# Softmax and squared-attention sums in a four-block transformer kernel: where their inverses are taken, and when statistics, sums and outputs are due

## What is computed

```python
x = x + squared_attention(_layernorm(x), Wq, Wk, Wv, Wo, gamma, beta)   # "squared"
x = x + gated_attention(_layernorm(x), W_gate, W_qkv)                   # "gated"
x = x + mqa_attention(_layernorm(x), Wqkv_w, Wqkv_b, out_w, out_b)      # "mqa"
x = x + gated_attention(_layernorm(x), W_gate, W_qkv)                   # "gated"
```

## Time and profile before

| | us |
|---|---|
| time before, median of 3 runs | 4368.68 (4368.31 to 4374.84) |
| the profiled execution's own time | 4371.04 |
| its span, first to last instruction | 4369.3 |
| PE busy | 3769.0 |
| POOL busy | 2965.8 |
| DVE busy | 1880.1 |
| ACT busy | 1638.2 |

### The profile page before, as it was taken

The page is one execution under the profiler, slowest core; times in us unless marked ns, Lnnn a source line. Parts: engine busy times, 40 slices in busy tenths (PEclk is TensorE's granted clock), DMA queues, the critical chain, the costliest instruction groups (busy, mean ns, idle before and its releaser), DMA issues. The chain is left out here.

```text
span 4369.3 us, 67371 instructions
## 1 busy us (share of the span) xinstructions
PE 3769.0 (86%) x26082; PEld 1520.9 (35%) x26082; DVE 1880.1 (43%) x4874; ACT 1638.2 (37%) x2433; POOL 2965.8 (68%) x2207
## 2 busy tenths in 40 slices
PE   7898998986989899898878878888898898998986
PEld 5343434332433333333333332333333333333332
DVE  1222222222555455455454444444454455555552
ACT  1544544552143333333434333333323333333343
POOL 2888787894076766767777666675565657666687
PEclk8999999998999999999999999999999999999998
DMA  1000100012010100101010010000100101000001
GB/s 68 15 15 22 37 20 30 11 59 73 10 30 1 59 1 23 37 1 40 20 32 28 11 37 13 27 32 15 44 1 15 44 1 59 1 23 27 1 29 40
DMA packets 63385, 115.08 MB, mean 26 GB/s; under 512 B 8673, under 2 KB 9185, under 8 KB 63073
## 3 DMA queue, kind: packets, MB, share of 16 engines
q1 hardware_dynamic: 63072, 110.77, 7.9%
HBM read 77.19 MB, written 33.55 MB: 25 GB/s over the span
## 5 line engine op out<-in xcount | busy, mean ns | idle before, releaser
L866 ACT ACTIVATE probs_soft<-banks 128x1024 f32<-128x1024 f32 (+1 forms) x960 | 848.3, 935 | 1339.8 <-PE banks L1171 1335.4
L774 POOL TENSOR_TENSOR added_soft<-added_soft,probs_soft 128x512 f32<-128x512 f32 (+1 forms) x380 | 1151.8, 3031 | 18.5 <-POOL added_soft L767 3.2
L959 DVE CUSTOM_DVE_ANT_0 banks<-banks,mask 128x128 f32<-128x128 f32 (+3 forms) x1536 | 701.3, 527 | 682.9 <-PE banks L1186 682.9
L954 DVE TENSOR_REDUCE maxima_soft<-banks 128x2 f32<-128x1024 f32 x384 | 452.4, 1221 | 503.3 <-PE banks L1186 503.3
L751 POOL TENSOR_SCALAR_AFFINE_SELECT probs_soft<-probs_soft 128x512 f32<-128x512 f32 x384 | 239.1, 635 | 568.6 <-ACT probs_soft L866 568.3
L1186 PE MATMUL banks<-k_soft,q_soft 32*128 32x512 f32 (+3 forms) x4608 | 508.8, 534 | 64.1 <-ACT probs_soft L866 63.6
L1139 PE MATMUL banks<-wide,xnT_soft 128*128 128x512 f32 x1024 | 500.6, 612 | 19.3 <-DVE picking_soft L938 11.0
L872 ACT ACTIVATE probs_squared<-banks,key_scale_squared 128x512 f32<-128x512 f32 (+3 forms) x768 | 378.9, 588 | 287.3 <-PE banks L1171 282.5
L1171 PE MATMUL banks<-q_soft,k_soft 32*128 32x512 f32 (+3 forms) x4608 | 481.2, 500 | 0.0
L1232 PE MATMUL banks<-probs_soft,v_soft 128*32 128x512 f32 (+3 forms) x4608 | 446.2, 507 | 10.2 <-DVE scaled_out_soft L1083 3.5
L774 POOL TENSOR_TENSOR added_squared<-added_squared,probs_squared 128x512 f32<-128x512 f32 (+1 forms) x124 | 376.9, 3039 | 5.1 <-POOL added_squared L774 1.4
(11 more groups left out here) (152 smaller groups left out, 4271.3 us busy)
## 6 DMA issues: line engine op xcount, KB each, us to landing
tiles_soft<-out SPq DMA_DIRECT2D x96, 256.0 KB, 2.7
rest_soft<-out SPq DMA_DIRECT2D x96, 256.0 KB, 2.9
out<-rest_soft SPq DMA_DIRECT2D x96, 256.0 KB, 2.1
tiles_squared<-in_x SPq DMA_DIRECT2D x32, 256.0 KB, 2.7
rest_squared<-in_x SPq DMA_DIRECT2D x32, 256.0 KB, 2.9
out<-rest_squared SPq DMA_DIRECT2D x32, 256.0 KB, 2.0
wide<-in_gated_wqkvT SPq DMA_DIRECT2D x3, 1024.0 KB, 7.7
raw_wq<-in_squared_wq SPq DMA_DIRECT2D x1, 1024.0 KB, 5.6
```

Of the source, the lines that this page charges most:

```text
L774: ins = pool.tensor_tensor(sums, sums, slot(ph, n)[:, :, col:col + width], ALU.add)
L866: ins = act.activation(slot(ph, n)[:, 2 * a:2 * a + 2, 0:width], score_pair(e, a)[:, :, 0:width], ACT.Exp, scale=SCALE)
L954: ins = dve.reduce_max(m["maxima"][:, ph % 2, 2 * a:2 * a + 2, t, p], score_pair(e, a)[:, :, col:col + width], AX_X)
L959: ins = dve.tensor_tensor_reduce(scores, scores, k["mask"][:, CHUNK - width:CHUNK], 1.0, MASKED, ALU.add, ALU.max, m["maxima"][:, ph % 2, ...
```

## The change

- `rs`, `widen` and `rw` go, and with them the transposes of sums and inverses. For gated and mqa phases VectorE takes reciprocals in place on `sums`, 128 columns at a time (`inv`, four for each chunk, in the half-steps after `sm`), and GpSimd multiplies 128x512 of `y` by them (`nrm`). Squared phases keep their `nrm` on VectorE.
- `out` of a gated stage no longer multiplies with inverses: VectorE adds the residual straight from PSUM, as in the other kinds; GpSimd's add goes. Every `out` now waits for `normalized`.
- `sm` comes one half-step later (16 and 10 instead of 15 and 9). Outputs 4 to 7 of a stage may not come before half-step 15, and the queue may pass over them.
- The statistics of the first four tiles of the next stage move from just before their `ln` in the stage's second phase into the projections of its first phase (`sprinkled`); those of tile t + 3 now come with `ln` of tile t. At most one `ln` is handed out in a half-step. The first four residual loads (`rload`), and for mqa the bias adds that go with them, move ahead of the next stage's tile loads.
- The mqa value bias is added by ScalarE as it evicts the products, not by VectorE later.
- The first four outputs of an act's last stage come one half-step later.

```diff
-SUMS_AT = (15, 9)
+SUMS_AT = (16, 10)
...
-        if t >= 2 and t + 2 < NT:
-            steps[-1].append(("stats", s, t + 2))
+        if t and t + 3 < NT:
+            steps[-1].append(("stats", s, t + 3))
...
+def sprinkled(work, some):
+
+    placed, first = list(work), len(work) // 3
+    for n in reversed(range(len(some))):
+        placed.insert(first + (len(work) - first) * n // len(some), some[n])
+    return placed
...
-    if kind == "gated":
-        return [(("rs", ph, c), 2)]
-    if kind == "mqa":
-        return [(("rs", ph, c), 2), (("widen", ph, c), 3), (("rw", ph, c), 4)]
+    if kind != "squared":
+
+        return [(("inv", ph, c, n), min(n + 1, 3 + c)) for n in range(TPC)] + [(("nrm", ph, c), 3 + c)]
     return [(("nrm", ph, c), 2)]
...
+    if event[0] == "out" and event[2] >= TPC:
+        return SUMS_AT[1] + 5
...
-        while queue and queue[0][1] <= n and (least * weight(queue[0][0], kinds) <= room or queue[0][2] <= n + 1):
-            room -= weight(queue[0][0], kinds)
-            events.append(queue.pop(0)[0])
-        carry = max(room, 0.0) if queue and queue[0][1] <= n else 0.0
+        while (x := due(queue, n)) is not None and (least * weight(queue[x][0], kinds) <= room or queue[x][2] <= n + 1):
+            if queue[x][0][0] == "ln" and normed:
+                break
+            normed = normed or queue[x][0][0] == "ln"
+            room -= weight(queue[x][0], kinds)
+            events.append(queue.pop(x)[0])
+        carry = max(room, 0.0) if due(queue, n) is not None else 0.0
...
+        head = ([("rload", s - 1, t) for t in range(TILES)] * (s > 0) + head[0], head[1])
...
-            work = [(head[0], 1), (parted(own[0]), HALVES - 2), (mixed(parted(outs[:half]), parted(own[1]), kinds), 2 * HALVES - 2)]
+            work = [(head[0], 1), (sprinkled(parted(own[0]), head[1]), HALVES - 2), (mixed(parted(outs[:half]), parted(own[1]), kinds), 2 * HALVES - 2)]
...
-            halves[-2] += parted(tail[:early])
-        work += [(head[1], 2 * HALVES - 2), (parted(merged), 2 * HALVES + 6), (parted(later + first), (3 if kinds[s + 1:s + 2] != ["squared"] else NG) * HALVES - 2),
+            halves[-1] += parted(tail[:early])
+        work += [(parted(merged), 2 * HALVES + 6), (parted(later + first), (3 if kinds[s + 1:s + 2] != ["squared"] else NG) * HALVES - 2),
...
+                elif u == "nrm" and soft:
+                    _, ph, c = e
+                    pool.wait_ge(sg.inverted, place["inv", ph, c, TPC - 1] + 1)
+                    wait_free(pool, ("av", ph, "AC"[c]))
+                    out = y_of(ph)[:, CHUNK * c:CHUNK * c + CHUNK]
+                    pool.tensor_tensor(out, out, m["sums"][:, c], ALU.mult).then_inc(sg.normalized, 1)
...
+                elif u == "inv":
+                    _, ph, c, n = e
+                    wait_free(dve, ("sm", ph, c))
+                    some = tile_of(m["sums"][:, c], n)
+                    dve.reciprocal(some, some).then_inc(sg.inverted, 1)
...
-                elif u == "rs":
-                    _, ph, c = e
-                    out = free(e)
-                    need(("sm", ph, c))
-                    for t in range(TPC):
-                        ins = pe.transpose(tile_of(out, t), tile_of(m["sums"][:, c], t), k["ident"][:])
-                    ready(e, ins)
-                elif u == "rw":
-                    _, ph, c = e
-                    out = free(e)
-                    pe.wait_ge(sg.widened, place["widen", ph, c] + 1)
-                    for t in range(TPC):
-                        ins = pe.transpose(tile_of(out, t), m["wide_inverse"][:, t].rearrange("p i d -> p (i d)"), k["ident"][:])
-                    ready(e, ins)
                 elif u == "out":
                     _, s, t = e
                     out = free(e)
                     for g in range(NG):
                         ph = NG * s + g
-                        if kind_of(s) == "gated":
-                            need(("av", ph, "AC"[t // TPC]))
-                        elif kind_of(s) == "mqa":
-                            need(("rw", ph, t // TPC))
-                        else:
-                            pe.wait_ge(sg.normalized, place["nrm", ph, t // TPC] + 1)
+                        pe.wait_ge(sg.normalized, place["nrm", ph, t // TPC] + 1)
```

More of the change, by code:

```diff
@@ L229, in mixed, with due @@
     return events
+def due(queue, n):
+    for x, (e, first, _) in enumerate(queue):
+        if first <= n:
+            return x
+        if "out" not in (e[0], e[1][0] if e[0] == "more" else ""):
+            return None
+    return None
 def spread(kinds, halves, rooms, work):
@@ L587, in act_program @@
     order = {name: [e for e in events if e[0] == name] for name in
-             ("load", "rload", "stats", "out", "mxr", "split", "krep", "vst", "ksq", "qsq", "kvar", "nrm", "rs", "widen", "rw", "gate")}
+             ("load", "rload", "stats", "out", "mxr", "split", "krep", "vst", "ksq", "qsq", "kvar", "inv", "nrm", "gate")}
     order["picks"] = [e for e in events if e[0] in ("kall", "vall")]
@@ L654, in stage_of @@
     def stage_of(e):
-        return e[1] // NG if e[0] in ("rs", "rw") else e[1]
+        return e[1]
     own_weights = OWN_WEIGHTS[soft]
@@ L709, in _ @@
                     _, s, t = e
-                    if kind_of(s) == "gated":
-                        sp.wait_ge(sg.summed, earlier("out", e, "gated") + 1)
-                    else:
-                        wait_free(sp, e)
+                    wait_free(sp, e)
                     stores[t % TILES].next()
@@ L895, in _ @@
                 elif u == "vs":
-                    take_out(e, m["v_parts"][:, e[2]], work[:, bank(e), :])
+                    take_out(e, m["v_parts"][:, e[2]], work[:, bank(e), :], weights["mqa"]["bv"][:, 0:1])
                 elif u == "gate_exp":
@@ L911, in _ @@
                     if ph:
-                        if soft:
-                            wait_work(act, ("rs", ph - 1, c))
-                        else:
-                            act.wait_ge(sg.normalized, place["nrm", ph - 1, c] + 1)
+                        act.wait_ge(sg.normalized, place["nrm", ph - 1, c] + 1)
                     take_out(e, m["sums"][:, c], work[:, bank(e), :], None if soft else k["eps2"][:, 0:1])
@@ L1023, in _ @@
                     ins.then_inc(sg.work_free[bank(e)], 1)
-                    wait_free(dve, e)
-                    dve.tensor_tensor(out, out, weights["mqa"]["bv"][:, None, :].broadcast_to([P, TPC, D]), ALU.add)\
-                        .then_inc(sg.biased_values, 1)
                 elif u == "v2":
@@ L1046, in _ @@
                     dve.tensor_tensor(out, work[:, bank(e), :], out, ALU.add).then_inc(sg.work_free[bank(e)], 1)
-                elif u == "nrm":
+                elif u == "inv":
[3 more added lines that the diff above has]
+                    dve.reciprocal(some, some).then_inc(sg.inverted, 1)
+                elif u == "nrm" and not soft:
                     _, ph, c = e
@@ L1054, in _ @@
                     dve.tensor_tensor(out, out, sums, ALU.mult).then_inc(sg.normalized, 1)
-                elif u == "rs":
-                    _, ph, c = e
-                    s, g = divmod(ph, NG)
-                    wait_work(dve, e)
-                    columns = work[:, bank(e), :].rearrange("p (t i d) -> p t i d", i=HG, d=D)[:, :, :, 0]
-                    if kind_of(s) == "gated":
-                        dve.reciprocal(m["inverse"][:, s % 2, TPC * c:TPC * c + TPC, HG * g:HG * g + HG], columns)\
-                            .then_inc(sg.work_free[bank(e)], 1)
-                    else:
-                        n = earlier("rs", e, "mqa")
-                        if n:
-                            dve.wait_ge(sg.widened, n)
-                        dve.reciprocal(m["few_inverse"][:], columns).then_inc(sg.work_free[bank(e)], 1)
-                elif u == "rw":
-                    _, ph, c = e
-                    out = y_of(ph)[:, CHUNK * c:CHUNK * c + CHUNK]
-                    wait_work(dve, e)
-                    wait_free(dve, ("av", ph, "AC"[c]))
-                    dve.tensor_tensor(out, work[:, bank(e), :], out, ALU.mult).then_inc(sg.work_free[bank(e)], 1)
                 elif u == "out":
@@ L1221, in _ @@
                         else:
-                            pe.wait_ge(sg.biased_values, place["vst", s, NC - 1] + 1)
+                            for half in range(NC):
+                                need(("vst", s, half))
                     if not soft:
```

64 lines of the change are left out of this document (14 added, 50 removed).

## The result

| | us | ratio to before |
|---|---|---|
| before, median | 4368.57 | |
| changed kernel, median of 4 runs (4027.61 to 4043.55) | 4031.91 | 0.923 [0.9209, 0.9252] |
| forecast | 4069 (3970 to 4190) | |

The kernel is 7.7% faster, 337 us. The forecast had 300 and the right sign. The profiled execution took 4027.61 us, its span is 4025.9.

The account below looks back on a forecast made before the run. TensorE's in-order list, with its waits, was taken as the bound. Gains of 384 us less costs of 84 gave 300 off the profiled 4371.0, so 4071, or 4069 for the median; range 3970 to 4190.

Parts of the forecast that it names:

- The costs: Sum of the predicted losses: 40 us for reciprocals, 36 for outputs waiting on `nrm`, 8 at the kernel's end; 84 us.
- Statistics, 105: TensorE's waits at `ln` for GpSimd's normalized tiles: earlier statistics remove 105 us of 153.9 (bounds 50 and 120).
- Clock, 45: TensorE's half-clock time after long `ln` stalls and `rw`'s waits: 45 us come back (bounds 20 and 90).
- Transposes, 153.4: `rs` and `rw` on TensorE: 70.3 + 83.1 us of busy time and idle ahead, all on the path and certain to go.
- Bank waits, 23: TensorE units waiting for a bank until VectorE has read `rs`'s columns: eleven wait entries, 23.0 us, gone.
- `sm`, 50: `sm` waiting for ScalarE's eviction after `av`: one half-step later, 50 of 57.9 us go.
- Outputs and the wait for `nrm`, +36 - 8: Outputs waiting for GpSimd's `nrm`: 3 us in each of 12 stages, cost 36 (0 to 108); gated `out` without GpSimd's add gains 8.
- the 8 us: Kernel's end: four quarters and a product after the last `sm`, first outputs a half-step later; cost 8 us (0 to 15).
- The quarters, 40: VectorE's 128-column reciprocals, 366 us of added work, delay row maxima TensorE waits for: cost 40 us (0 to 366).
- the first rival: More comes back: clock stays up (90 instead of 45), gaps take all quarters, `nrm` on time; about 3985 us, chance 0.18.
- The second rival: VectorE's list fills in half-steps 11 to 14, TensorE waits some 2 us more in 48 phases; about 4165 us, chance 0.15.
- the rival in which GpSimd is held: `nrm` on GpSimd waits for VectorE's fourth quarter, adds and masks queue behind, TensorE stops; 4465 us at one add, chance 0.03.

## Why the prediction came out as it did

The time lies inside the range, 37 us below the forecast, and the bound was read rightly: TensorE's list, with the waits in it. The costs were put too high, 84 us, and that is where the 37 us come from. The sum's terms against what was found:

**Statistics, 105.** The waits fell by 117.8 (153.9 to 36.1); taking the part back costs 118 in time. The doubt that a half-step may not cover an add was not needed: after the openings 3.7 us remain (2.6 in the second act, 1.1 in the first). Loads that now come behind the residual loads made nobody later: VectorE's waits for loaded tiles fell from 40.0 to 29.0 us.

**Clock, 45.** TensorE was busy at half clock for 272.0 us before and is for 147.6 now; half of the difference, 62 us, is what the clock gave back, 5 of it on the transposes. The rest is 54 to 57, depending on how overlaps are counted, so the mechanism holds and the size was 10 us too small. (Taking the 88.3 us of the transposes' rows from the 120.7 would leave only 32.4, but those rows overlap others, see below.)

**Transposes, 153.4, "all on the path and certain to go".** They went, with their waits. But two steps were wrong. The rows' 88.3 us of busy time overlap neighbouring instructions: only 67.1 us are time in which nothing else kept TensorE busy, so 21 us of the term could never come back. And "on the path" failed as a rule: put back without waits, 62.9 us of them cost 29. TensorE's 91% is not a path without slack in this kernel; a row of busy time doesn't give what its removal brings. The 65.1 us of idle time ahead of them are gone from the view. No run brings `widen` and `rw` back, so what these 83.1 us were worth in time isn't shown.

**Bank waits, 23, and `sm`, 50.** The former are gone; `sm` has 4.5 us left of 57.9, so 53.4. The run with `sm` back is 106 us slower, so the edit was worth more than its row. Of the 112 us between the two profiled executions 54 are these waits, 37 are longer busy time, which is clock, and 21 are other waits that rise with the quarters and the product a half-step earlier. Which of the three moves takes the clock isn't shown.

**Outputs and the wait for `nrm`, +36 - 8.** `out` in the gated stages waits 31.6 us in all. For GpSimd's product it waits twice, 13.6 us, and both times are in the last stage, where the outputs stand right behind the product. In the other eleven stages of the second act the step that put 3 us in each was wrong. The product does come late there, 1.1 to 5.8 us after the fourth quarter, behind masks, bias adds or statistics; but TensorE gets to the outputs only 0.4 to 6.7 us after the product's end. At the end of the kernel the 8 us were about right: from the last scoring instruction to the end it is 25.0 us before and 30.5 now, 5.5 more, although 13.6 us of waits lie in it.

**The quarters, 40.** With the 36 us for `nrm` the most wrong term. Waits for maxima rose by 9.0 us (54.2 to 63.2), taking most of the quarters' work away brings 8 or nothing. I had read the gaps (399 of them, 3.0 us each) and yet priced the quarters as a share of VectorE's time. The share is not a constant: 0.92 us in a gap is nearly free, double that for each of the 384 costs 168 us. So the first rival had two of its three reasons right, the gaps and the product on time; the clock gave back less than its 90. Its sum was wrong: with `nrm` on time it should have come to 3948, below the range, as it left out that term's 36 us. The second rival, VectorE filling locally, holds at twice the quarters.

**Unforeseen.** The split of the maxima is late on GpSimd, 20 times, 19.5 us more than before; the text said what is queued behind the product ("the next add and the masks") and left out the split, for which TensorE waits three half-steps later. One run that reorders it wins 16 us. And in the squared phases `av` waits 19.5 us for masks (10.7 before). The moved statistics are not the main cause: with them alone the wait is 10.6 us, and with them taken back it is still 17.3. Which edit it is stays open. What does come with them is a wait for GpSimd's squares of the keys (L1263), 5.5 us: none before, the same 5.5 with the part alone, 2.7 with it taken back.

**The whole, and luck.** In the profiled executions the terms nearly close. Idle time lost 117.8 + 65.1 + 23.0 + 53.4 = 259.3 us and got back 9.0 (maxima), 19.5 (split) and 13.6 (last outputs); that is 217 of 222.7. Busy time lost 67.1 of transposes and 53.6 of clock. So the gains were 380 where 384 were forecast, which is partly luck: the transposes were 21 too high, statistics and clock 13 and 9 too low. The costs were some 42 where 84 were forecast. Nor do the terms add up as times: taken back one by one, the statistics cost 118 us for 108.7 of waits, `sm` with what follows it 106 for 54, and the transposes 29 for 62.9 of work.

**How the trace bears out the rest.** The marks set for "right" held, or the trace was better than they: the waits at `ln` are 36 us where 50 were expected, those for maxima 63 and not 80 to 110, and the clock is 0.974 for 0.965 or more. TensorE's busy time is 3648 us for about 3635, since the overlap of the transposes was left out. The reciprocals don't contend with GpSimd, 890 to 954 ns each; and the rival in which GpSimd is held has one wait of 13.8 us for a quarter, at the very end of the kernel. The Trainium skill's advice of tiles of 512 elements or more ("VectorE: DVE Perf Modes", on the TRN2 errata) would have cost 63 us here. What "Perfetto Trace Analysis" of the Trainium skill says on optimizing Scalar/DVE operations, to break up instructions where an engine isn't saturated but causes bubbles on others, is what the runs bear out.

## What to carry to other kernels

Look in the wait view for work that is late only because it stands right ahead of its reader in an in-order list, and start it a phase earlier; here that was about a third of the gain (101 us alone, 118 in the changed kernel), with no work added to any engine. When you add work to an engine that isn't the bound, compare the length of one piece with the gaps ahead of its critical instructions, and then how many gaps the pieces fill in all: in this kernel four pieces of 0.92 us were nearly free, one of 3.35 us cost 63, and four pairs of 0.92 us cost 168. When you take instructions from a busy engine, don't read what they were worth from their row; put them back alone and measure (here 29 us for a row of 62.9). And before you move something on an in-order engine, list all that stands behind it, down to small steps with a reader soon after.

## What was not expected of the hardware

- Four quarters back to back take 3.39 us together at the end of the kernel, against 3.35 for one instruction of 512 columns; 384 of them have a mean of 919 ns where I had 952. In busy time the quarters take 337.6 us and the whole chunks of that experiment 321.0, so cutting costs 16.6 us over the kernel and not the 44 I worked out: neighbours overlap.
- A product of two SBUF operands on VectorE beside a busy GpSimd has a mean of 1805 ns with a minimum of 691 and a maximum of 4986; in that run all 58 that took longer began while a GpSimd instruction ran, and none of the 38 short ones did. In the squared phases, where nothing about it was edited, the mean rose from 1666 to 2457 ns: 17 of 32 took 0.69 us before and 5 now, and all longer ones again began while a GpSimd instruction ran.
- The run in which TensorE waits 78 times for 0.75 us at `sm` is 106 us slower for 54 us more of such waits, and 37 us of the rest are longer busy time at a lower clock. The quarters and products moved too in it, so that the short waits alone are not shown to cost it.
